# Attention in a language-model tower: four banks of scores, three single banks of maxima reduced 512 columns at a time, and weighted values for 512 queries in one call

## The reference, cut to what matters

```python
attn = jnp.einsum('bhqd,bhkd->bhqk', query, key) / scale      # 64 (batch, head) pairs, 2048 x 2048 scores each
attn = jax.nn.softmax(attn, axis=-1)
out = jnp.einsum('bhqk,bhkd->bhqd', attn, value)
```

## Time and profile before

| | us |
|---|---|
| median of 3 runs (lowest to highest) | 3354.92 (3351.03 to 3359.83) |
| the profiled execution's own time | 3353.22 |
| its span in the profile | 3351.2 |
| PE busy in the span | 3220.0 |
| DVE busy | 2888.2 |
| ACT busy | 2468.3 |
| POOL busy | 572.2 |

### The profile page before, as it was taken

One profiled execution on the slowest core, in us unless ns is written; L12 is line 12 of the kernel. 1 busy time (PEld: TensorE's weight loads), 2 busy tenths in 40 slices (PEclk: granted clock), 3 DMA queues, 4 the chain that ended last, 5 costly groups with the idle time before them and its releaser, 6 DMA issues. The chain is left out here.

```text
span 3351.2 us, 67576 instructions
## 1 busy us (share of the span) xinstructions
PE 3220.0 (96%) x27520; PEld 1381.0 (41%) x27520; DVE 2888.2 (86%) x3156; ACT 2468.3 (74%) x4578; POOL 572.2 (17%) x753
## 2 busy tenths in 40 slices
PE   7997999999999999999999999999999999986998
PEld 3443333333333333333333333333333333375665
DVE  5778999999999999999999999999999999375232
ACT  3431788888888888888888888888888888832221
POOL 7882000000000000000000000000000000065233
PEclk9997899999999999999999999999999999987999
DMA  6895222131313131313131222212222220078662
GB/s 197 243 296 160 45 61 57 55 69 39 71 37 71 37 74 37 74 37 71 40 84 38 71 46 62 51 58 51 60 48 58 45 83 21 30 260 275 213 221 97
DMA packets 250466, 305.40 MB, mean 91 GB/s; under 512 B 45013, under 2 KB 177662, under 8 KB 244780
## 3 DMA queue, kind: packets, MB, share of 16 engines
q1 hardware_dynamic: 238124, 271.63, 29.1%
q0 software_dynamic: 12032, 29.45, 2.7%
HBM read 165.81 MB, written 139.23 MB: 91 GB/s over the span
## 5 line engine op out<-in xcount | busy, mean ns | idle before, releaser
L1016 DVE TENSOR_REDUCE max_parts<-ps_m 128x2 f32<-128x1024 f32 x2048 | 2486.9, 1224 | 82.9 <-PE ps_m L866 75.3
L1001 ACT ACTIVATE probs<-ps_s 128x512 f32<-128x512 f32 x4096 | 2217.0, 597 | 308.6 <-PE ps_s L897 115.1
L866 PE MATMUL ps_m<-keys,queries 48*128 48x512 f32 x4096 | 1484.9, 453 | 18.7 <-DVE max_parts L1016 18.7
L897 PE MATMUL ps_s<-queries,keys 51*128 51x512 f32 x4096 | 1479.1, 446 | 12.6 <-DMA queries<-neg_rows 3.4
L914 PE MATMUL ps_o<-probs,vals 128*32 128x256 f32 x16384 | 1295.5, 391 | 0.0
L897 PEld LDWEIGHTS ps_s<-queries,keys 51*128 51x128 f32 x4096 | 610.0, 185 | 837.0 <-issue 790.2
L866 PEld LDWEIGHTS ps_m<-keys,queries 48*128 48x128 f32 x4096 | 596.7, 187 | 78.1 <-DVE max_parts L1016 51.6
L914 PEld LDWEIGHTS ps_o<-probs,vals 128*32 128x32 f32 x16384 | 329.4, 108 | 719.0 <-issue 697.6
L822 POOL TENSOR_TENSOR heads_out<-weighted,recip_rows 128x512 f32<-128x512 f32 x63 | 80.8, 1283 | 2145.3 <-DMA recip_rows<-recip_rows_dram 2145.3
L1646 DVE TENSOR_TENSOR hidden<-ps_u,silu 128x320 f32<-128x320 f32 x64 | 31.5, 492 | 136.4 <-PE ps_u L1578 136.4
L1622 ACT ACTIVATE silu<-ps_g 128x320 f32<-128x320 f32 x64 | 28.0, 438 | 147.6 <-PE ps_g L1578 147.6
(11 more groups left out here) (108 smaller groups left out, 1563.8 us busy)
## 6 DMA issues: line engine op xcount, KB each, us to landing
slot_rows<-empty SPq DMA_DIRECT2D x16, 1290.0 KB, 5.2
rows_d<-slot_rows SPq DMA_DIRECT2D x16, 1290.0 KB, 8.5
vext<-val SPq DMA_DIRECT2D x64, 256.0 KB, 4.9
halves_q<-parts SPq DMA_DIRECT2D x64, 256.0 KB, 3.7
halves_k<-parts SPq DMA_DIRECT2D x64, 256.0 KB, 3.1
keys<-halves_k SPq DMA_DIRECT2D x32, 512.0 KB, 7.9
queries<-halves_q SPq DMA_DIRECT2D x128, 128.0 KB, 3.3
vals<-vext SPq DMA_DIRECT2D x32, 512.0 KB, 5.6
```

Of the source, the lines that this page charges most:

```text
L866: mm = pe.matmul(ps_m[m % 2][:, h, :], queries_r[par][rows, qt, p, t * P:(t + 1) * P], keys_r[par][rows, p, c * 512:(c + 1) * 512], start= ...
L897: pe.matmul(ps_s[bank][:], keys_r[par][rows, p, k * P:(k + 1) * P], queries_r[par][rows, qt, p, :], start=True, stop=True).then_inc(scores ...
L1001: act.activation(probs[:, n % RING, :], ps_s[bank][:], ACT.Exp, scale=SCALE).then_inc(probs_ok[bank], 1)
L1016: dve.tensor_reduce(max_parts[:, lu % 2, :, p, t, c], ps_m[m % 2][:], AX.X, ALU.max).then_inc(maxima_ok[m % 2], 1)
```

## The change

The eight banks of PSUM are dealt out anew, 4 for scores, 3 x 1 for maxima and 1 for weighted values. A maximum is now a tile of its own: `tile` counts them, each has a bank `tile % 3`, PE waits before each one for the reduction of three tiles ago, and DVE reduces 512 columns per instruction. `weigh` takes all 512 queries in one call at the end of a group. Two semaphores of the start (`ones_set`, `half_set`) become one.

```diff
-        self.maxima_ok = [sem(f"maxima_ok{i}") for i in range(2)]
-        self.probs_ok = [sem(f"probs_ok{i}") for i in range(3)]
+        self.maxima_ok = [sem(f"maxima_ok{i}") for i in range(3)]
+        self.probs_ok = [sem(f"probs_ok{i}") for i in range(4)]
...
-    BANKS = 3
+    BANKS = 4
+    MBANKS = 3
...
-        ps_m = [ctx.enter_context(nc.psum_tensor(f"ps_m{i}", [P, 2, CH], F32)) for i in range(2)]
+        ps_m = [ctx.enter_context(nc.psum_tensor(f"ps_m{i}", [P, CH], F32)) for i in range(MBANKS)]
...
-                if h and not (n < 0 and m < 2):
-                    pe.wait_ge(maxima_ok[m % 2], step * (MAXIMA // 2) + m // 2)
+                tile = 2 * (step * MAXIMA + m) + (1 - h)
+                if tile >= MBANKS:
+                    pe.wait_ge(maxima_ok[tile % MBANKS], tile // MBANKS)
...
-                mm = pe.matmul(ps_m[m % 2][:, h, :], queries_r[par][rows, qt, p, t * P:(t + 1) * P],
+                mm = pe.matmul(ps_m[tile % MBANKS][:], queries_r[par][rows, qt, p, t * P:(t + 1) * P],
                                keys_r[par][rows, p, c * 512:(c + 1) * 512], start=True, stop=True)
-                if h == 0:
-                    mm.then_inc(maxima_ps, 1)
+                mm.then_inc(maxima_ps, 1)
...
-            def weigh(step, n, at, half):
+            def weigh(step, n, at):
...
-                    mm = pe.matmul(ps_o[32 * j:32 * j + 32, cols], vals[:, par, k, VW * j:VW * (j + 1)],
-                                   probs[:, (n + j) % RING, cols], start=k == 0 and half == 0, stop=k == KT - 1 and half == 1)
-                if half:
-                    mm.then_inc(pv_ok[n // QUAD % SLOTS_PV], 1)
+                    mm = pe.matmul(ps_o[32 * j:32 * j + 32, :], vals[:, par, k, VW * j:VW * (j + 1)],
+                                   probs[:, (n + j) % RING, :], start=k == 0, stop=k == KT - 1)
+                mm.then_inc(pv_ok[n // QUAD % SLOTS_PV], 1)
...
-                        halves = (0, 1) if k == LAG and half else () if k == LAG else (half,)
-                        for part in halves:
-                            if n >= LAG * QUAD:
-                                weigh(step, n - LAG * QUAD, at, part)
-                            elif not first:
-                                weigh(step - 1, TILES + n - LAG * QUAD, PLACES[0], part)
+                    if n >= LAG * QUAD:
+                        weigh(step, n - LAG * QUAD, at)
+                    elif not first:
+                        weigh(step - 1, TILES + n - LAG * QUAD, PLACES[0])
...
-                dve.wait_ge(maxima_ps, step * MAXIMA + m + 1)
-                dve.tensor_reduce(max_parts[:, lu % 2, :, p, t, c], ps_m[m % 2][:], AX.X, ALU.max).then_inc(maxima_ok[m % 2], 1)
+                for h in (1, 0):
+                    tile = 2 * (step * MAXIMA + m) + (1 - h)
+                    dve.wait_ge(maxima_ps, tile + 1)
+                    dve.tensor_reduce(max_parts[:, lu % 2, h, p, t, c:c + 1], ps_m[tile % MBANKS][:], AX.X, ALU.max).then_inc(maxima_ok[tile % MBANKS], 1)
```

More of the change, by code:

```diff
@@ L251, in phase_a @@
         half_set = stage.half_set
-        ones_set = sem("ones_set")
         stats_raw = sem("stats_raw")
@@ L379, in _ @@
             root(0, 0)
-            pool.memset(val[:], 1.0).then_inc(ones_set, 1)
+            pool.memset(val[:], 1.0).then_inc(half_set, 1)
             first_heads.fill(pool)
@@ L577, in _ @@
             dve.wait_ge(tables_in, 32)
-            dve.wait_ge(ones_set, 1)
+            dve.wait_ge(half_set, 4)
             def chunk(b, k, last):
@@ L904, in weigh @@
                 bank = at[0][n + QUAD - 1]
[L905 to L908, removed]
+                pe.wait_ge(probs_ok[bank], step * PER_BANK[bank] + at[1][n + QUAD - 1] + 1)
+                if k == 0:
                     pe.wait_ge(weighted_ok, step * UNITS + lu)
@@ L965, in _ @@
             for n in range(TILES - LAG * QUAD, TILES, QUAD):
-                for half in range(2):
-                    weigh(STEPS - 1, n, PLACES[1], half)
+                weigh(STEPS - 1, n, PLACES[1])
         @block.scalar
@@ L1014, in reduce_max @@
                 p, t, c = g // (QT * KC), g // KC % QT, g % KC
-                dve.wait_ge(maxima_ps, step * MAXIMA + m + 1)
-                dve.tensor_reduce(max_parts[:, lu % 2, :, p, t, c], ps_m[m % 2][:], AX.X, ALU.max).then_inc(maxima_ok[m % 2], 1)
+                for h in (1, 0):
+                    tile = 2 * (step * MAXIMA + m) + (1 - h)
+                    dve.wait_ge(maxima_ps, tile + 1)
+                    dve.tensor_reduce(max_parts[:, lu % 2, h, p, t, c:c + 1], ps_m[tile % MBANKS][:], AX.X, ALU.max).then_inc(maxima_ok[tile % MBANKS], 1)
                 if g == MAX_UNIT - 1:
-                    dve.wait_ge(maxima_ok[m % 2], step * (MAXIMA // 2) + m // 2 + 1)
+                    dve.wait_ge(maxima_ok[tile % MBANKS], tile // MBANKS + 1)
                     if not (isinstance(step, int) and step * UNITS + lu < 2):
@@ L1220, in _ @@
             pool.memset(no_mean[:], 0.0).then_inc(half_set, 1)
-            pool.wait_ge(half_set, 6)
+            pool.wait_ge(half_set, 7)
             pool.wait_ge(proj_ps, 1)
@@ L1287, in _ @@
             pe.wait_ge(const_in, 16 * NCONST)
-            for i in range(2):
-                pe.wait_ge(attention.maxima_ok[i], QUADS * (SEQ // CH) * (SEQ // P))
+            tiles = 2 * QUADS * (SEQ // CH) * (SEQ // P) * 2
+            for i in range(3):
+                pe.wait_ge(attention.maxima_ok[i], (tiles - i + 2) // 3)
             project(0, 0)
```

## The result

| | us | ratio to the kernel before |
|---|---|---|
| kernel before, median | 3353.74 | |
| changed kernel, median of 4 runs | 3567.89 (3566.18 to 3569.91) | 1.0641, 95% interval 1.0625 to 1.0657 |
| span in the profile, before and after | 3351.2 and 3564.3 | |

A forecast was written before the change was run, and what follows sets the result against it. PE leads before, DVE close behind; after, a closed chain of 2.70 us a group binds. Units give +187.5 us, maxima ahead +2.9, last groups -4: +186 on 3353.2, so 3539 to 3540 us, range 3438 to 3620.

The forecast's parts named there:

- The chain: Phase B: first reduction, fourth maximum, weighted values, next first maximum, next reduction close a loop of 2.70 us a group; chance 0.76.
- The short reductions: DVE's 512-column reductions: 0.69 us long, 0.60 apart, 2.40 us a group; rival without overlap, 2.76 us, 3615 us, chance 0.08.
- The same page's price for one reduction: Trainium skill's 0.66 us for 512 columns out of PSUM in place of 0.69: chain 2.67 us, sum about 3509 us.
- Weighted values in one call: PE at a group's end: two passes of 512 columns take 1.00 us, as in group LAG, against 2 x 0.57 before.
- The last link: Next group's first maximum with its own load exposed, 0.50 us, and 0.04 us to DVE's start.
- the turn: Once a unit: 0.59 us of PE work before the fourth maximum, 0.36 of it hidden by the chain, 0.2 us staying.
- The maxima done ahead: Maxima ahead of the units: 84 reductions x 0.60 instead of 42 x 1.13, +2.9 us, DVE leading.
- The last groups: Last 21 groups, without maxima, 2.18 us each: each loses one change to weighted values, 0.14 to 0.27, together -4 us.
- the fourth reduction: In a group, counted from the first reduction's start: ends at 1.28 us at the earliest, or behind the others at 2.49.
- the weight loads' wait: Sign in the changed profile: PEld waits for the reduction about 1000 times, some 0.3 us each.
- The clock: PE's granted clock in phase B: left at 1.00 although PE pauses about 0.3 us at a time; named as possible error.
- Group LAG: Group where PE waits behind the copy of ps_o: four banks of scores save its 0.36 us.

The follow-up runs named there:

- cols256: Changed kernel, each reduction reading only 256 of its bank's 512 columns, matmuls, banks and order unchanged: 3300.46 us, ratio 0.9832 to the kernel before.
- twice: Changed kernel with the third maximum's matmul of each group issued twice into its bank: 3569.7 us, ratio 1.0635 to the kernel before.
- banks34: Changed kernel with four single banks of maxima and three of scores in place of three and four: 3506.04 us, ratio 1.0431 to the kernel before.
- halves: Changed kernel with weighted values again in two calls, one after each half group, the rest kept: 3351.98 us, ratio 0.9985 to the kernel before.
- split_only: Kernel before, each pair of maxima reduced by two instructions of 512 columns in place of one of 1024: 3359.5 us, ratio 1.0012.
- once_only: Kernel before, weighted values in one call of 512 queries at the end of a group, banks as before: 3506.7 us, ratio 1.0441.
- swap: Changed kernel with the maximum issued ahead of the score in each group's first pair: 3533.83 us, ratio 1.0532 to the kernel before.

## Why the prediction was right

*The chain.* It was the forecast's decisive step, and it holds link by link: 0.75, 0.43, 1.00 and 0.56 us in the trace for 0.74, 0.42, 1.00 and 0.54, together 2.74 for 2.70. It is shown by more than the trace. Shortening one link by 0.27 us shortened the group by 0.27 (`cols256`); work in the gap of the chain was free (`twice`); another bank for the maxima moved the wait to the scores, at 2.61 us (`banks34`); opening the chain with two calls took back everything (`halves`).

*The short reductions.* Forecast 0.69 us long and 0.60 apart, measured 0.68 to 0.69 and 0.60. `split_only` confirms that they cost nothing under PE's 2.46 us. At 0.60 us from start to start each reduction begins before the one in front of it has ended. The Trainium skill ("VectorE: DVE Perf Modes", the section on the DRAIN) says that the next operation waits for an empty pipeline, and adds that one that is not held starts earlier; the prediction told only the first half, which would have put them 0.69 apart, and the runs agree with the second. The same page's price for one reduction (the section on the TRN2 errata), 0.66 us, is near the length and would have made the sum 3509 us, farther off.

*Weighted values in one call.* Forecast 1.00 us, taken from group LAG, measured 0.99 to 1.00.

*What was too small.* The sum missed 28 us of 214. The last link was short by 0.03 us, a signal that comes late behind another one, and the other links by 0.01 together: 0.04 x 1003 groups = 40 us. Against it stood the turn, for which I had 0.2 us a unit, 12 us in all, and which the trace shows almost free: in the changed kernel its group runs from 1565.31 to 1568.09, 2.78 us.

```profile
1565.31 0.50 PE L867 MATMUL ps_m<-keys,queries 48*128 48x512 f32 x1
...
1566.71 0.40 PE L867 MATMUL ps_m<-keys,queries 48*128 48x512 f32 x1
1567.10 1.07 PE L912 MATMUL ps_o<-probs,vals 128*32 128x512 f32 x8
1568.09 0.50 PE L897 MATMUL ps_s<-queries,keys 51*128 51x512 f32 x1
```

There the fourth maximum starts 1.40 us after the first without having waited, and the weighted values follow it in 0.39 us, not 0.43, with the weights loaded ahead. The maxima done ahead were priced at +2.9 us, and from their first matmul to the first score it is 58.0 us instead of 54.8 (284.7 to 342.7 us, against 288.4 to 343.2). That price was right, and yet the first score came no later, because this work began 3.7 us sooner; no run here tells why. The last groups were priced at -4, measured -3.3. So the total is as close as it is partly by luck: 40 us too little in the chain, 12 too much in the turn.

*Two slips that changed nothing.* The 1.28 us after which the fourth reduction was said to end is where it could start; it stands behind the others and ends at 2.49 us, as computed and as in the trace. And the weight loads' wait, announced with 0.3 us, is 0.7 us each; 0.3 is PE's own standstill.

*The clock.* It was left at 1.00, and phase B of the changed kernel kept it. `once_only` and `banks34` were forecast in the same way, and there it fell in the last groups.

*Group LAG.* I said that four banks of scores save its 0.36 us. Inside the changed kernel that can't be told from the chain, which sets this group like any other. `halves` shows that the saving would have been 0.1 us even with the chain open elsewhere, because it stays closed there. It changed nothing in the sum.

## What to carry to other kernels

When buffers go round between two engines, write the chain from a buffer's release to the next use of the same place and add it up with latencies, not with start-to-start distances; compare that with each engine's total work. A long instruction or call that nothing else may pass belongs to every chain that crosses it: merging two such calls saved 0.14 us of work a group and yet made the group 0.28 us longer, since three banks no longer bridged it. Where such a chain binds, an engine's spare time is worth nothing (`twice`); a shorter link helps (`cols256`, `swap`), or the long call cut in two (`halves`), or one more buffer on that side, as long as it isn't taken from another ring that then closes a chain of its own (`banks34`).

## What the runs showed of the hardware

The two matmuls of a pair start and end within 0.01 us of each other and signal two engines. The engine of the first starts about 0.04 us after its matmul's end, that of the second about 0.07: in the changed kernel that was ACT and then DVE, in `swap` DVE and then ACT. I had expected both at 0.04.

In `once_only` and `banks34`, PE's granted clock fell to 0.50 in the last groups, and the groups grew from 2.61 to 4.07 us. In `banks34` the groups without maxima begin at 3002.0 us, and for some 14 us more the clock stayed:

```profile
core 0: us, PE busy (x) PEld busy (x) DVE busy (x) ACT busy (x) POOL busy (x), PEclk, DMA share, GB/s
3004.00:3016.00 12.00, 10.39 (x60) 3.01 (x52) 0.00 (x0) 9.39 (x20) 0.00 (x0) 1.00 0.31 113
```

PE was busy for 87% of that stretch, with one pause of about 0.45 us in most groups, and then the clock fell. In phase B of the changed kernel PE was busy for 88% (2394.16 of 2710 us), with one pause of 0.34 us a group, and the clock stayed at 1.00. So the profile's busy share alone does not tell the two apart. The 94% of `once_only` (60.83 of 65 us) were measured after the fall, when every matmul took longer. The changed kernel's last groups, which mostly take 1.96 to 2.12 us, kept 1.00.
